# Score mask added by GpSimd after the weighting, in place of TensorE's mask matmuls, in a local-attention and mixture-of-experts kernel

## What is computed

```python
xn = _layernorm(x)
attn = einsum('bhnd,bhmd->bhnm', q, k) * scale      # q, k, v from xn @ qkv_w.T
m = _local_mask(WINDOW, Nn)                          # (w - |i-j|/2) / w in the window, else 0
attn = jnp.where(m != 0.0, attn * m, -jnp.inf)
attn = jax.nn.softmax(attn, axis=-1)
s = einsum('bhnm,bhmd->bhnd', attn, v) ... @ proj_w.T + proj_b
g = _silu(ffn(xn))                                   # argmax router, sigmoid score, 8 experts, shared expert
x = x + s * g
```

## Time and profile before

| | us |
|---|---|
| median of 3 runs | 673.12 |
| lowest and highest | 670.14, 675.69 |
| profiled execution, its own time | 672.93 |
| its span, first to last instruction | 670.9 |
| TensorE busy in it | 624.8 |
| VectorE busy | 441.2 |
| ScalarE busy | 301.5 |
| GpSimd busy | 185.9 |

### The profile page before, as it was taken

One profiled execution on the slowest core, in us unless ns is written; L12 is line 12 of the kernel. 1 busy time (PEld: TensorE's weight loads), 2 busy tenths in 40 slices (PEclk: granted clock), 3 DMA queues, 4 the chain that ended last, 5 costly groups with the idle time before them and its releaser, 6 DMA issues.

```text
span 670.9 us, 11700 instructions
## 1 busy us (share of the span) xinstructions
PE 624.8 (93%) x4020; PEld 550.1 (82%) x4020; DVE 441.2 (66%) x903; ACT 301.5 (45%) x573; POOL 185.9 (28%) x160
## 2 busy tenths in 40 slices
PE   2599999997999999999999999999999989899986
PEld 1478898887888998888998898899888767888885
DVE  6748667975574453555355445356699999987883
ACT  1453634666534434433533633543636353654340
POOL 5001111386720010001000100001655555531320
PEclk9989989997999999999999999999999999999995
DMA  9232220032254555554555456432323333320010
GB/s 294 93 114 82 80 75 13 27 102 82 90 164 149 163 172 156 171 169 147 172 171 182 142 171 179 145 124 74 107 75 106 118 93 106 120 82 14 29 33 21
DMA packets 74297, 77.24 MB, mean 115 GB/s; under 512 B 6520, under 2 KB 71808, under 8 KB 74240
## 3 DMA queue, kind: packets, MB, share of 16 engines
q1 hardware_dynamic: 65408, 62.88, 30.6%
q0 software_dynamic: 3072, 8.39, 4.0%
q10 hardware_dynamic: 5760, 5.25, 2.4%
HBM read 51.58 MB, written 18.87 MB: 105 GB/s over the span
## 4 chain that ended last, share of the span: by engine, by line
PE 72%; DVE 17%; ACT 4%; issue 4%; another core or an unknown queue 1%; DMA 1%; DVEq 0%
PE psV L936 13%; PE psM L985 11%; PE psS L909 10%; PE psM L962 7%; PE psT L918 5%; PE psM L994 4%; PE psM L943 4%; PE psM L886 3%; PE psM L926 3%; PE psM L957 3%; DVE O L752 3%; PE psS L906 3%; DVE X L792 2%; DVE Sx L712 2%; PE psM L891 2%
## 5 line engine op out<-in xcount | busy, mean ns | idle before, releaser
L426 POOL TENSOR_TENSOR Sx<-Sx,mx 128x752 f32<-128x752 f32 x64 | 93.7, 1464 | 441.9 <-DVE mx L719 441.7
L936 PEld LDWEIGHTS psV<-VB,PTs 128*128 128x128 f32 x1024 | 123.7, 196 | 4.7 <-ACT PTs L469 1.9
L936 PE MATMUL psV<-VB,PTs 128*128 128x64 f32 x1024 | 124.4, 276 | 2.5 <-DVE O L752 2.4
L909 PE MATMUL psS<-kBD,qBD 128*128 128x188 f32 x512 | 106.0, 332 | 0.0
L909 PEld LDWEIGHTS psS<-kBD,qBD 128*128 128x128 f32 x512 | 88.7, 196 | 10.4 <-issue 2.8
L752 DVE TENSOR_TENSOR O<-psV,rs 32x128 f32<-32x128 f32 x256 | 71.9, 281 | 37.3 <-PE psV L936 26.3
L712 DVE TENSOR_TENSOR Sx<-psS,cst 128x752 f32<-128x752 f32 x64 | 60.1, 939 | 46.4 <-PE psS L909 41.3
L469 ACT ACTIVATE PTs<-psT 128x1024 f32<-128x1024 f32 x64 | 65.4, 1022 | 37.3 <-PE psT L918 28.6
L985 PE MATMUL psM<-xT,EB 128*128 128x128 f32 x640 | 79.5, 277 | 1.6 <-ACT kBD L469 1.6
L985 PEld LDWEIGHTS psM<-xT,EB 128*128 128x128 f32 x640 | 75.8, 192 | 4.4 <-ACT kBD L469 3.6
L726 DVE SCALAR_TENSOR_TENSOR ea<-et,psM 128x256 f32<-128x256 f32 x40 | 16.8, 421 | 81.8 <-ACT et L535 81.8
(11 more groups left out here) (110 smaller groups left out, 803.1 us busy)
## 6 DMA issues: line engine op xcount, KB each, us to landing
EB<-in_L_ffn_gate_w SPq DMA_DIRECT2D x40, 256.0 KB, 2.9
EB<-in_L_ffn_up_w SPq DMA_DIRECT2D x40, 256.0 KB, 3.2
EB<-in_L_ffn_down_w SPq DMA_DIRECT2D x40, 256.0 KB, 2.9
xs_dram<-blank SPq DMA_DIRECT2D x10, 512.0 KB, 4.8
stage<-xs_dram SPq DMA_DIRECT2D x40, 128.0 KB, 4.4
ys_dram<-yb ACTq DMA_DIRECT2D x40, 128.0 KB, 2.8
EB<-in_L_attn_x SPq DMA_DIRECT2D x16, 256.0 KB
out<-EB SPq DMA_DIRECT2D x16, 256.0 KB, 2.2
```

The lines of the kernel that those rows point to most:

```text
L426: nc.gpsimd.tensor_tensor(s, s, mx[n % 3][:, :].unsqueeze(2).broadcast_to([P, 2 * G, KW]), ALU.subtract).then_inc(a_sub, 1)
L909: last = mm(psS[:, i, j * HS * KW:(j + 1) * HS * KW], qBD[h % 2][:, j, k, :, :].rearrange("p s q -> p (s q)"), kBD[h % 2][:, j, :, k * QB: ...
L936: last = mm(rows[:, g // HS, :, g % HS, :], PTs[n % 2][:, g, :], VB[n % 2][:, :, g * VC:(g + 1) * VC], start=True, stop=True)
```

## The change

TensorE no longer writes the mask: the two products of each block start a fresh accumulation. The float32 mask of the constants moves to the part of them that stays in SBUF, its kinds are reordered (first, inner, last) so that the kinds of a step's two blocks are neighbours, and a new GpSimd instruction `banded(n)` adds it to the weighted scores in place. `largest(n)` waits for that sum in place of `weigh(n)`. On VectorE `largest(n)` moves from directly behind `weigh(n)` to behind `total(n-2)`, and `total` gets a wait on the reciprocal of the step before. On GpSimd `banded(n)` stands ahead of `subtract(n)`, behind `combine` and behind all the scatters or gathers of step n-1. The bfloat16 tiles and their two casts go, with the waits on them.

```diff
-c[:, C_MASK:] = np.concatenate([...(band, band & (key >= WIN), band & (key < QB + WIN))])
+c[:, C_MASK:C_MASK + 3 * KW] = np.concatenate([...(band & (key >= WIN), band, band & (key < QB + WIN))])
...
-            nc.gpsimd.tensor_copy(identb[:, :], ident).then_inc(s_cast, 1)
-            nc.gpsimd.tensor_copy(maskb[:, :, :, :], maskf.unsqueeze(2).broadcast_to([P, 3, G, KW])).then_inc(s_cast, 1)
...
+            def banded(n):
+                pool.wait_ge(a_mul, n + 1)
+                s = Sx[n % 3][:, :, :].rearrange("p (g i) k -> p g i k", i=2)[:, :, :, 0:KW]
+                first, second = (mask_kind(block_of(n, i)) for i in range(2))
+                kinds = mask[:, first:second + 1, :].unsqueeze(1).broadcast_to([P, G, 2, KW])
+                nc.gpsimd.tensor_tensor(s, s, kinds, ALU.add).then_inc(a_add, 1)
...
                 if n < U:
+                    banded(n)
                     subtract(n)
...
             def largest(n):
-                dve.wait_ge(a_mul, n + 1)
+                dve.wait_ge(a_add, n + 1)
...
             def total(n):
                 dve.wait_ge(a_exp, n + 1)
+                if n >= 1:
+                    dve.wait_ge(a_rec, n)
...
                 if n < U:
                     weigh(n)
-                    largest(n)
...
                 if 0 <= n - 2 < U:
                     total(n - 2)
+                if n < U:
+                    largest(n)
...
             def scores(n):
-                if n == 0:
-                    pe.wait_ge(s_cast, 2)
...
-                    mm(psS[:, i, 0:BW], identb[:, :], maskb[:, mask_kind(block), :, :]..., start=True, stop=False)
                     for j in range(KC):
-                        last = mm(psS[...], qBD[...], kBD[...], start=False, stop=j == KC - 1)
+                        last = mm(psS[...], qBD[...], kBD[...], start=True, stop=True)
```

More of the change, by code:

```diff
@@ L8 @@
 F32 = mybir.dt.float32
-BF16 = mybir.dt.bfloat16
 I32 = mybir.dt.int32
@@ L62 @@
 C_HEAD = C_BIAS + C
-C_STAY = C_HEAD + HS
+C_MASK = C_HEAD + HS
+C_STAY = C_MASK + 3 * KW
 C_TRI, C_ONE = C_STAY, C_STAY + P
@@ L66 @@
 C_TILE = C_FIRST + E
-C_MASK = C_TILE + NT
-C_END = C_MASK + 3 * KW
+C_END = C_TILE + NT
 def constants(bias):
@@ L85, in constants @@
     key = np.arange(KW)[None, :]
-    kinds = (band, band & (key >= WIN), band & (key < QB + WIN))
-    c[:, C_MASK:] = np.concatenate([np.where(k, 0.0, NEG) for k in kinds], 1)
+    kinds = (band & (key >= WIN), band, band & (key < QB + WIN))
+    c[:, C_MASK:C_MASK + 3 * KW] = np.concatenate([np.where(k, 0.0, NEG) for k in kinds], 1)
     return c
@@ L96, in mask_kind @@
     at = block % (SEQ // QB)
-    return 1 if at == 0 else 2 if at == SEQ // QB - 1 else 0
+    return 0 if at == 0 else 2 if at == SEQ // QB - 1 else 1
 def key_pieces(n):
@@ L236, in build @@
         ones = rcst[:, C_ONE - C_STAY:C_ONE - C_STAY + P]
-        maskf = rcst[:, C_MASK - C_STAY:].rearrange("p (m k) -> p m k", m=3)
+        mask = cst[:, C_MASK:C_MASK + 3 * KW].rearrange("p (m k) -> p m k", m=3)
         psS = ctx.enter_context(nc.psum_tensor("psS", [P, 2, 512], F32))
@@ L249, in build @@
         s_x = [sem(f"s_x{i}") for i in range(len(GROUPS))]
-        s_const, s_wq, s_ws, s_wr, s_fill, s_zero, s_cast = (
-            sem("s_" + n) for n in ("const", "wq", "ws", "wr", "fill", "zero", "cast"))
+        s_const, s_wq, s_ws, s_wr, s_fill, s_zero = (
+            sem("s_" + n) for n in ("const", "wq", "ws", "wr", "fill", "zero"))
         s_dve, s_bn, s_var, s_sqrt = (sem("s_" + n) for n in ("dve", "bn", "var", "sqrt"))
@@ L257, in build @@
         m_full = [sem(f"m_full{i}") for i in range(MB)]
-        a_qk, a_S, a_mul, a_max, a_sub, a_exp, a_T, a_PT, a_V, a_PV, a_sum, a_rec, a_nrm, a_OT, a_s = (
-            sem("a_" + n) for n in ("qk", "S", "mul", "max", "sub", "exp", "T", "PT", "V", "PV", "sum", "rec", "nrm", "OT", "s"))
+        a_qk, a_S, a_mul, a_add, a_max, a_sub, a_exp, a_T, a_PT, a_V, a_PV, a_sum, a_rec, a_nrm, a_OT, a_s = (
+            sem("a_" + n) for n in ("qk", "S", "mul", "add", "max", "sub", "exp", "T", "PT", "V", "PV", "sum", "rec", "nrm", "OT", "s"))
         x_v = [sem(f"x_v{i}") for i in range(2)]
@@ L380, in _ @@
                     sp.wait_ge(r_tab, 1)
-                    sp.wait_ge(s_cast, 2)
                     for i in range(2):
@@ L905, in scores @@
                     k = block % (HALF // QB)
-                    mm(psS[:, i, 0:BW], identb[:, :], maskb[:, mask_kind(block), :, :].rearrange("p g k -> p (g k)"),
-                       start=True, stop=False)
                     for j in range(KC):
                         last = mm(psS[:, i, j * HS * KW:(j + 1) * HS * KW], qBD[h % 2][:, j, k, :, :].rearrange("p s q -> p (s q)"),
-                                  kBD[h % 2][:, j, :, k * QB:k * QB + KW], start=False, stop=j == KC - 1)
+                                  kBD[h % 2][:, j, :, k * QB:k * QB + KW], start=True, stop=True)
                 last.then_inc(a_S, 1)
```

2 lines of the change are left out of this document (removed).

## The result

Over 20 runs each, the changed kernel takes 675.09 us (673.6 to 680.7) and the kernel before 673.02 us (666.62 to 677.45). The ratio of the means is 1.0063, with a 95% interval of 1.0035 to 1.009: a slowdown of 0.6%, within the 1% that the prediction calls the same. It leaves out two slow executions of the kernel before (677.43 and 677.45 us, over 1.5% above its fastest); the medians of all runs lie only 0.3% apart. The profiled execution took 675.92 us with a span of 674.1 us.

The account below looks back on a forecast made before the run. TensorE was taken to bound the kernel, except VectorE between 485 and 586 us. Late by 6.8 us at `weigh(54)`, then -2.6 + 0.5, gives +4.7 on 672.93: 677.6, put down as 677 us, range 665 to 689.

Parts of the forecast that it names:

- Mask matmuls: Two matmuls a step on TensorE go: 0.16 us each, 0.32 us a step, 20.5 us at most.
- The addition: One new GpSimd addition of 752 elements a step, between weighting and maximum: 1.80 us, bounds 1.46 and 1.88.
- Steps 0 to 9: TensorE sets the pace: gain 3.2 us, less 1.2 us charged for the later maximum, so 2.0 us early.
- Scatter stage: Steps 10 to 16: GpSimd needs 10.55 us a step, TensorE waits for `divide`; loss of 12.7 us.
- SyncE's late rows: SyncE's first expert rows wait for the last scatter, some 14 us later; all but 0.7 us hidden.
- Steps 18 to 41: TensorE sets the pace and slack takes the addition's delay: gain 24 x 0.32 = 7.7 us.
- Steps 42 to 54: Last arithmetic: GpSimd's loop of 8.0 us plus collisions in two of eight steps, 8.3 a step, 99.6 us.
- To the end: Steps 55 to 62 gain 2.6 us on TensorE; the last chain with the addition costs 0.5 us.
- (b): Rival: collisions stay in the last arithmetic, 9.2 us a step, +11 us, 688 us; chance 0.20.
- (c): Rival: full gain, as GpSimd idles 441.7 us and nothing waits: 652 us; chance 0.03.
- (d): Rival: the mask was free, filling time of the scores' weight loads, so no gains: 690 us; chance 0.07.
- (a): Rival: cheap addition of 1.45 us and `combine` never meets VectorE: 667 us; chance 0.15.

Follow-up runs that it names:

- no_mask: The kernel before with TensorE's mask matmuls left out and nothing in their place: 655.45 us, ratio 0.984.
- mask_moved: The changed kernel with the mask 141 numbers further on in the constants' tile: 682.8 us in one execution.
- order_free: The kernel before with VectorE's new order and without TensorE's mask matmuls, no addition on GpSimd: 648.05 us, ratio 0.970.
- scatter_between: The changed kernel with one of five scatters of each of steps 10 to 15 moved between the next step's addition and subtraction: 667.09 us, ratio 1.001.
- pe_scatter: The changed kernel with TensorE's mask matmuls and no addition in steps 10 to 17 alone: 661.78 us, ratio 0.990.
- add_only: The changed kernel with TensorE's mask matmuls kept in all steps and GpSimd adding zeros: 693.97 us, ratio 1.040.
- order_only: The kernel before with only VectorE's new order, TensorE's mask kept, no addition on GpSimd: 655.31 us, ratio 0.981.
- old_order: The changed kernel with VectorE's maximum put back directly behind the weighting: 708.44 us, ratio 1.063.
- pe_both: The changed kernel with TensorE's mask matmuls and no addition in steps 10 to 17 and 40 to 55: 650.29 us, ratio 0.974.

## Why the prediction was right, point by point

The forecast was 677 us against a measured ratio that makes 677.2 us of its base of 672.93; direction and size hold. That they agree to 0.2 us is luck: the interval of the ratio is 3.7 us wide, the medians are 2.1 us apart and not 4.2, and in the sum errors cancelled. Lateness against the kernel before, in us, at the marks of the prediction:

| mark | forecast | in the trace |
|---|---|---|
| `weigh(10)` | -2.0 | -3.6 |
| scores of step 18 | +10.7 | +7.3 |
| `weigh(42)` | +7.1 | +3.3 |
| `weigh(54)` | +6.8 | +4.6 |
| end | +4.7 | +3.2 |


- **Mask matmuls, 0.32 us a step.** Right: 0.31 in steps 20 to 40 (no_mask). Where it pays was right as well: not in steps 40 to 56.
- **The addition, 1.80 us, bounds 1.46 and 1.88.** It took 1.55 us. The scaling from `combine` was the wrong guide in this kernel; by place alone the value can be 1.80 (mask_moved). 0.25 us less in 19 steps should have taken 4.8 us off the forecast.
- **Steps 0 to 9.** Expected 2.0 us early at `weigh(10)`, found 3.6. Given how the start of step 10 wanders, this says little; the charge of 1.2 us isn't visible.
- **Scatter stage.** The chain was right link by link: GpSimd's unbroken turn, VectorE held by the maximum, TensorE released by `divide`. Expected turn 10.55, found 10.26 with the shorter addition; expected loss 12.7 us from `weigh(10)` to the scores of step 18, found 72.3 - 61.4 = 10.9 us between the same marks. The shorter addition explains both, with 7 x 0.25 = 1.75 us less of loss and a turn of 10.30. Against order_free, a kernel without the addition but otherwise the same, the stage loses 14.4 us. scatter_between and pe_scatter show that it is GpSimd's row and that the loss isn't given back. Steps 18 to 20 take 17.7 us, against 17.4 in order_free, which leaves room for a part of the 0.7 us charged for SyncE's late rows; no run shows them apart.
- **Steps 18 to 41.** Right, the addition hidden (add_only).
- **Steps 42 to 54, 99.6 us.** Found 101.2. The size fits, the working does in part. The prediction charged a collision in two of eight steps, and three in twelve are what is left; but it said that the others go since GpSimd's new loop moves `combine`. The order alone does that (order_only, -7.7 us in W without any addition), so there was a gain of 7.7 us to be had before the addition took 8.9 (order_free to changed). And GpSimd's loop of 8.0 us was computed with an addition of 1.80; with 1.55 it should be 7.75, and is 7.9 to 8.0, for the gathers take 1.05 us on average in place of 0.97. On top came the long turn by ScalarE, 2.7 us, which no step of the prediction had: it costed the later `exps` at nothing, which is right, but did not look at ScalarE's wait for `combine`. So 3.0 us too much for the addition stood against 2.7 for that turn and some 2 us for the gathers and the rest.
- **To the end.** From `weigh(54)` on it expected 2.1 us less (-2.6 + 0.5), and 1.4 us less were found.
- **The rivals.** (b), collisions that stay, is what old_order shows, with 9.8 us a step. (c), full gain, did not come, and GpSimd's unbroken row is the reason for the scatter stage only; pe_both comes near its 652 us, but by leaving the addition out of 24 steps and with the order's gain, which (c) did not have. (d) is out. (a) needed a cheap addition and no collisions; the addition was nearly as cheap, but three collisions stayed, and the turn by ScalarE and the longer gathers came on top.

The miss worth learning from is in how the parts were cut. The diff moves a VectorE instruction and adds a GpSimd one, and the prediction treated the move as a device to hide the addition. It never asked what the move does alone, though the earlier trace rows showed the collision that the move removes, and `combine`'s start hangs on the maximum through `subtract`. The move alone gives 1.9% at no cost, the cheapest gain in the whole case.

The Trainium skill ("SBUF — State Buffer", § Who interferes with whom) says that a VectorE instruction with two SBUF inputs and a GpSimd instruction that reads SBUF shut each other out for the whole instruction. The traces agree in both senses: `result` takes 2.31 us beside `combine` in old_order, and 0.68 us in order_only, where `combine` falls on the weighting, which has one input in PSUM. The prediction knew the rule, and used it for the addition and for where `combine` falls in the changed kernel as a whole, but never for the move taken alone.

## What to carry to other kernels

Split a diff that moves work and adds work, and cost each part alone; a move also shifts when another engine runs, and so what it collides with. Work can be handed to an engine that idles on average only in the stages where its own row has gaps: here the addition was hidden in 40 steps of 64, as far as the traces tell, and cost nearly all of its 24 us in the other 24. Where a stage is full, keep the old way for that stage alone: that version took 0.974 of the time, while the uniform change took 1.006.

## What the runs showed of the hardware

- A GpSimd addition of 752 float32 elements took 1.55 us with its second operand at one place of a tile (changed kernel) and 1.80 us 564 bytes further on (mask_moved), on the same data, each the mean of 64 instructions. Most of the single ones lie near 1.52 or 1.66 us in the first kernel and near 1.65 or 1.81 in the second, by the part of the mask that they read. I had not expected that a place in SBUF matters to GpSimd. What about the place matters wasn't tried.
- The scatter stage of the changed kernel, in which TensorE was busy for 57.24 of 68 us, ran at a mean granted clock of 0.87, against 0.94 before (56.65 of 60); the expert stage, where it was busy for 273.17 of 277 us, ran at 1.00, as before.
- GpSimd's indirect gathers took 1.05 us on average in the changed kernel and 0.97 before. That comes with VectorE's new order and not with the addition: they take 1.07 us in order_only and 0.97 in old_order. The longer ones (1.25 us) ran beside two-input instructions of VectorE, but so did some of the short ones; whether these are the cause wasn't tested.
